# Attention masks of a graph network: one edge column per instruction, the lane row minus one scalar compared with a second

## What is computed

```python
for l in range(2):
    q, k, v = ...                                   # per node, 8 heads of 16
    att = einsum('ehd,ehd->eh', q[dst], k[src]) / 4
    ex = exp(clip(att) - m[dst])
    alpha = ex / segment_sum(ex, dst)[dst]
    aggr = segment_sum(v[src] * alpha[:, :, None], dst)
    x = x + aggr @ Wo[l] + bo[l]
    x = x + gelu(layernorm(x) @ W1[l] + b1[l]) @ W2[l] + b2[l]
```

## Time and profile before

| | |
|---|---|
| median of 3 runs | 7770.34 us (7765.22 to 7776.23) |
| the profiled execution's own time | 7750.4 us |
| its span | 7748.6 us |
| granted TensorE clock, mean | 0.769 |
| attention passes (first bf16 mask at 4671.0 us to the end) | about 3080 us of the span |
| visits of groups in them | 488, with 976 halves of masks |

### The profile page before, as it was taken

The page is one execution under the profiler, slowest core; times in us unless marked ns, Lnnn a source line. Parts: engine busy times, 40 slices in busy tenths (PEclk is TensorE's granted clock), DMA queues, the critical chain, the costliest instruction groups (busy, mean ns, idle before and its releaser), DMA issues.

```text
span 7748.6 us, 113775 instructions
## 1 busy us (share of the span) xinstructions
PE 4792.9 (62%) x23913; PEld 3787.7 (49%) x23914; DVE 4147.9 (54%) x11534; ACT 1234.6 (16%) x2992; POOL 4644.2 (60%) x4895
## 2 busy tenths in 40 slices
PE   2345555566665566765445666777777776766666
PEld 1334444344544444554344455655655555555555
DVE  8235666224454134444223556777666667766666
ACT  0000000000000000000000012333333333333333
POOL 0677764677763777763777776764433257654441
PEclk9956666688887788887556777888777878788887
DMA  1222211333332333321222223322211123322211
GB/s 43 62 52 55 57 49 38 89 105 109 109 95 63 104 105 106 101 86 49 53 52 59 61 60 95 101 86 70 63 58 56 36 85 101 88 71 66 59 57 27
DMA packets 254924, 558.68 MB, mean 72 GB/s; under 512 B 78725, under 2 KB 127104, under 8 KB 254842
## 3 DMA queue, kind: packets, MB, share of 16 engines
q0 software_dynamic: 200704, 514.10, 23.8%
q10 hardware_dynamic: 46284, 35.32, 1.4%
q1 hardware_dynamic: 7854, 8.31, 0.4%
HBM read 522.11 MB, written 35.31 MB: 72 GB/s over the span
## 4 chain that ended last, share of the span: by engine, by line
PE 33%; POOL 24%; DVE 17%; issue 15%; ACT 4%; DVEq 3%; DMA 2%; POOLq 0%; SPq 0%; ACTq 0%
POOL ring L973 24%; PE acc_ps L1246 12%; PE bank L1203 8%; PE acc_ps L1218 5%; ACT mask_t L999 3%; PE bank L1195 2%; PE bank L1294 2%; DMA ring<-rows,idx_stage 2%; DVE dots L674 2%; PE bank L1186 1%; PE bank L1352 1%; DVE early L411 1%; DVE wide L671 1%; DVE rows L637 1%; DVE mask_bf L545 1%
## 5 line engine op out<-in xcount | busy, mean ns | idle before, releaser
L973 POOL DMA_INDIRECT ring<-rows,idx_stage x4704 | 4595.7, 977 | 2781.9 <-issue 1717.3
L1246 PE MATMUL acc_ps<-ring,mask 128*128 x7808 | 2045.1, 424 | 1735.9 <-SPq L921 930.1
L1246 PEld LDWEIGHTS acc_ps<-ring,mask 128*128 128x128 f32 x7808 | 1586.4, 255 | 2178.5 <-issue 2039.9
L545 DVE SCALAR_TENSOR_TENSOR mask<-dst_f,neg_first,lane 128x256 f32<-128x256 f32 x1952 | 932.7, 485 | 2148.3 <-PE acc_ps L1246 2045.0
L1203 PE MATMUL bank<-own,mask_t 128*128 (+1 forms) x3904 | 861.8, 355 | 586.5 <-ACT mask_t L999 484.5
L1203 PEld LDWEIGHTS bank<-own,mask_t 128*128 128x128 f32 x3904 | 648.3, 236 | 760.2 <-ACT mask_t L999 317.6
L1218 PE MATMUL acc_ps<-msg,mask 128*128 128x136 f32 x3904 | 725.4, 345 | 4.1 <-DVE msg L688 4.1
L1218 PEld LDWEIGHTS acc_ps<-msg,mask 128*128 128x128 f32 x3904 | 679.8, 254 | 4.7 <-issue 4.7
L545 DVE SCALAR_TENSOR_TENSOR mask_bf<-dst_f,neg_first,lane 128x256 f32 x976 | 473.4, 485 | 317.0 <-PE bank L1353 198.4
L999 ACT ACTIVATE mask_t<-bank 128x256 f32<-128x256 f32 x976 | 374.0, 383 | 1505.6 <-PE bank L1195 1502.8
L671 DVE TENSOR_TENSOR wide<-bank,ring 128x256 f32<-128x256 f32 x976 | 393.5, 422 | 235.1 <-PE bank L1203 153.5
(11 more groups left out here) (188 smaller groups left out, 3885.8 us busy)
## 6 DMA issues: line engine op xcount, KB each, us to landing
ring<-rows,idx_stage POOLq DMA_INDIRECT x4704, 2.7
rows<-own ACTq DMA_DIRECT2D x48, 256.0 KB
rows<-wide ACTq DMA_DIRECT2D x48, 256.0 KB
rows<-own ACTq DMA_DIRECT2D x26, 128.0 KB
rows<-own ACTq DMA_DIRECT2D x1, 3136.0 KB
out<-own ACTq DMA_DIRECT2D x24, 128.0 KB
w_ff<-in_L_gnn_W SPq DMA_DIRECT2D x4, 256.0 KB
w<-in_L_gnn_W SPq DMA_DIRECT2D x2, 256.0 KB
```

Of the source, the lines that this page charges most:

```text
L545: return vec.scalar_tensor_tensor(out=to, in0=dst_f[:, bass.ds(col + 2 * h, 2)].unsqueeze(2).broadcast_to([P, 2, P]), scalar=neg_first[:, ...
L973: pool.indirect_dma_start(ring[:, j, 0:WIDTH[p]], None, tables[p][:, :], bass.IndirectOffsetOnAxis(ap=idx_stage[:, half, j:j + 1], axis=0) ...
L1246: ins = pe.matmul(to, mask[:, j, :], rhs, start=False, stop=final and j == GC - 1)
```

## The change

Instead of one `scalar_tensor_tensor` for two columns, which broadcasts `dst_f` along the lanes and `lane` over the two columns, each column gets a `tensor_scalar` of its own: `lane_bf` minus the partition's `dst_f`, compared with the partition's `neg_first`. Both scalars are read from SBUF, one value per partition. The input and the output are now both bf16. The masks of the convolutions are written as before.

```diff
                 a = visit(p - CONVS, sweeps, t, g)
-                make_mask(mask_bf[:, bass.ds(a & 1, 1), 2 * h:2 * h + 2, :].rearrange("p a c n -> p (a c) n"),
-                          t, g, back, h).then_inc(mask_bf_ready, 1)
+                col = nc.s_assert_within((g + 1 - back) * GC, 0, COLS,
+                                         skip_runtime_bounds_check_because="the ranges end with the sweep's last group")
+                for j in (2 * h, 2 * h + 1):
+                    ins = vec.tensor_scalar(mask_bf[:, bass.ds(a & 1, 1), j, :].rearrange("p a n -> p (a n)"), lane_bf[:, :],
+                                            dst_f[:, bass.ds(col + j, 1)], neg_first[:, bass.ds(t, 1)],
+                                            ALU.subtract, ALU.is_equal)
+                ins.then_inc(mask_bf_ready, 1)
```

## The result

The changed kernel takes 7866.25 us in the median (7863.77 to 7873.77, 4 runs) against 7767.78 us for the kernel before, a ratio of 1.0127 with a 95% interval of 1.0109 to 1.0144. It is slower by 98 us, where 28 were forecast, and lies outside the range. The two executions that were profiled lie 117 us apart (7750.4 and 7867.0 us), so differences read from the two traces add up to 117 and not to 98.

The account below looks back on a forecast made before the run. VectorE and TensorE were taken to chase each other, the leader depending on TensorE's clock. 16 us for `dots` and 12 for masks gave 28 us on the median 7770.3, 7798 us (+0.36%), range 7758 to 7845.

Parts of the forecast that it names:

- What bounds the kernel: Attention passes: VectorE and TensorE lead by turns; longer VectorE work is hidden at the low clock, not the high one.
- The price of the new instruction: One-column mask on VectorE: 310 ns each, two starting 0.22 us apart.
- GpSimd's share: GpSimd lengthening the new masks: 0.015 us added per pair, so a half's end comes 0.06 us later.
- What follows the first half: From first mask to `wide`: 0.45 us grows by 0.15, upper bound 0.22, lower 0.045.
- What follows the second half: From the second half's mask to `msg`: about 0.01 us later, costed at nothing.
- What reaches TensorE: Delays that pass on to TensorE: (a) and (b) together, 28 us; waits take up the addition in the remaining visits.
- (a): TensorE's q matmuls released by `dots`: 106 visits, each 0.15 us later, 16 us.
- (b): TensorE's turning matmul released by a mask: 203 waits, each 0.06 us later, 12 us.
- The clock: Rival, 6%: later masks idle TensorE at high clock; twenty visits fall to the low level, 44 us, 7842 in all.
- Hidden: Rival, 28%: VectorE's extra time falls into slack everywhere, 7770 to 7785 us.
- faster: Rival, 11%: paired new masks overlap, under about 0.10 us apart, 7753 us; or packing outweighs fixed parts, 7730.
- No packing: Rival, 7%, with much locking: new masks at upper bounds, over 0.38 us each, adding 73 us, 7843.

Follow-up runs that it names:

- e4: e1 with only the second half of each visit's masks written one column at a time: 8083.77 us, +55 over e1.
- e12: The changed kernel with loaded ranges masked to 14 bits and four unread matmuls after each turned half: 7716.85 us, ratio 0.9936.
- e11: The kernel before with loaded ranges masked to 14 bits and four unread matmuls after each turned half: 7678.45 us, ratio 0.9889.
- e3: e1 with only the first half of each visit's masks written one column at a time: 8101.34 us, +73 over e1.
- e9: The kernel before with loaded ranges masked to 14 bits: 7825.97 us, ratio 1.0068.
- e10: The changed kernel with loaded ranges masked to 14 bits: 7890.43 us, ratio 1.0162.
- e1: The kernel before with run-time bounds checks on the loaded group ranges: 8028.39 us, ratio 1.0341.
- e13: e9's kernel with an idle VectorE instruction that delays only `wide` by 0.15 us: ratio 1.0071 to the kernel before.
- e16: e11's kernel with eight unread matmuls in place of four: ratio 0.9935 to the kernel before.
- e5: The same kernel as e9, in a comparison where the kernel before was slow: ratio 1.0049.

## Why the prediction was wrong

**What bounds the kernel.** Right: VectorE and TensorE lead each other by turns, and what was slowed on VectorE was not hidden.

**The price of the new instruction.** Right: 310 ns and 0.22 us apart were forecast, 314 (median) and 0.23 measured. The four elements a cycle that the Trainium skill gives for it in "VectorE: DVE Perf Modes", section "The perf-mode tier table (the rule you actually need)", fit, if its fixed part is that of L770; no run measures the two parts apart. The saving did not help, as forecast. VectorE's busy time grew by 91 us and not by 130: the forecast added two durations for a pair (0.62 us) where the pair covers 0.54.

**GpSimd's share.** Too small: 15 ns were set for a pair. Mean less median is 335 - 314 = 21 ns for each of the two, 42 for a pair, and nearly all of it comes from the 231 instructions that ended with one of GpSimd. A half's masks took 0.485 us before; now they take 0.537 in the median and in the mean 0.568 (first half) and 0.589 (second), 0.08 and 0.10 us later where 0.06 was priced.

**What follows the first half.** 0.60 us to `wide` was forecast, 0.63 measured there and 0.62 in the median of all visits: 0.17 to 0.18 later than before, between the 0.15 that was taken and the upper bound of 0.22.

**What follows the second half.** This was costed at nothing, with `msg` about 0.01 us later. Where nothing else holds `msg`, it now starts 0.03 us later behind `logits` (0.63 us against 0.60), and in the mean of all visits 0.07 us later (1.06 against 0.99). That e4, which has only this half, costs 55 us says that the place is not free; how much of it is `msg` and how much the later masks stays open.

**What reaches TensorE.** The step "(a) and (b), 28 us" had the right places and was too small. The wait for `dots` grew by 28 us (forecast 16) and that for masks by 18 (12), and the number of visits in them grew as well, 106 to 142 and 203 to 216; the sum had taken the old counts as fixed. VectorE's wait for q rows gave back only 14 us of the 35 forecast; its wait for landed gathers, which the forecast left out, gave back 29 (78.1 to 48.8). With the clock held equal the direct cost is 38 us (e12 - e11), so this step alone would have been no bad miss.

**The step that failed** is the one that was not a term at all: the sum added delays at a fixed clock, and kept "granted clock 0.81 in the attention passes". It went to 0.77, which is one of the signs of being wrong that the prediction named (a move of more than 0.01), with TensorE busy for 101 us longer over the attention passes (2268 against 2168, same instructions). The clock stood among the rivals with 6% and a price of 44 us, twenty visits at 2.2. The time at the low clock grew by 257 us (1194 to 1451), which at 5.7 us a visit is some 45 visits, more than twice the twenty. The price of one was too high in turn: 5.7 less 3.5 took a single fast visit, and between `msg` and `msg` the medians are 5.55 us wholly at the low clock and 4.08 at the high one, 1.5 apart. 45 x 1.5 is 67 us as an estimate, and with the 38 of the direct part 105. The rival asked for an idle gap in one place; what came was a third more falls, most without a gap of 1 us.

That empty time lowers the clock, and costs, is shown by the fillers (147 and 174 us). That the change's own loss goes the same way is shown in part. TensorE's longer work makes up 101 of the 117 us between the two original traces and 13 of 40 with the clock held up, and the cost falls from 64 to 38 us when it is held, but by an amount with a wide interval. What in the change sets it off (late products, late masks, or the exclusion beside GpSimd) stays open: e3 and e4 say only that either half is enough, and theory P was not tested on its own, though the trace shows that the exclusion is there.

**The rivals.** "Hidden" is out by the 98 us, and "faster" also by its own sign: the two like instructions start 0.23 us apart, not 0.09. "No packing" is out by the 314 ns.

## What to carry to other kernels

Where TensorE runs in bursts between waits for other engines, a delay of 0.1 us on another engine may cost more than its length: look at the granted clock of the stretch first. If it is well under 1, as the 0.81 here, further idle time can lower it, and matmuls that fill the waits, in a bank that TensorE owns, are worth a try; here they gained 147 us of 7826 in one setting and 23 of 10160 in another. Splitting one VectorE instruction of 256 elements into two of 128 did not win by a faster mode, since two new ones start 0.23 us apart, most of which is fixed. Price an engine's delay at the counts of waits that it will create, not at those that are there. And read from two traces TensorE's busy and idle time apart: the same instructions taking longer point at the clock.

## What was not expected of the hardware

The clock's falls need no long pause, as told above. Between the two original traces more of the loss lay in the second attention layer (85 us, 0.81 to 0.75) than in the first (32 us), with the same instructions in both. That is no property of the layers: between e9 and e10 the two layers, parted at the last `msg` of the first, lose 33 and 30 us.

The same program took 7766 us in some comparisons and 10091 to 10139 in others. It isn't known to be a matter of the chip: the chip numbered 7 is on record with 7765 us beside e1 to e4 and with 10091 beside e13 to e16. e9 and e5 are the same kernel, on either side, with equal VectorE work (4151 and 4152 us) and a granted clock of 0.760 and 0.689. In e5 TensorE's work takes 407 us longer, and GpSimd's nearly equal work is 45% of the span instead of 59%; first e9, then e5:

```profile
PE 4872.5 (62%) x23913; PEld 3845.0 (49%) x23914; DVE 4151.2 (53%) x11534; ACT 1234.8 (16%) x2992; POOL 4659.5 (59%) x4895
```

```profile
PE 5279.9 (52%) x23913; PEld 4173.8 (41%) x23914; DVE 4151.7 (41%) x11534; ACT 1214.8 (12%) x2992; POOL 4592.5 (45%) x4895
...
PEclk9655556667776667777556676777777766677667
```

What makes it slow was not looked for.
